# A graph network in one kernel: narrower count in layer 2, key tile, node parts, store and copies of the last layers

## The chip, the cores and the metric

One core of a Trainium2 chip runs the whole program in one launch. The metric is device microseconds from start to end of an execution; three executions give a median. One more execution was taken by the hardware profiler, and all rows below are from it.

## The reference

6250 nodes with 32 features, 200000 edges sorted by target. Four graph layers, each with a residual and a layer norm. Shapes come from the kernel's inputs.

```python
x = _layernorm(x + L0(x, edge_attr_32))     # relu(x[src] + e), summed over dst
x = _layernorm(x + L1(x))                   # cosine attention, softmax over dst
x = _layernorm(x + L2(x, edge_attr_2))      # spline convolution
x = _layernorm(x + L3(x, edge_attr_16))     # five PNA sub-layers
# L2: keys = row * 25 + idx[:, s]; four basis weights s, h summed by key, then
out = jnp.einsum('nki,kio->no', h, weight) / clip(deg, 1) + x @ root_weight + bias
# L3, five times, T = 4 towers of 8 features:
h = einsum(concat([xi, xj, ee]), pW) + pb   # xi = x[dst], xj = x[src], ee = edge_attr @ eW + eb
ssum = segment_sum(h, dst); cnt = segment_sum(1, dst)
mean = ssum / max(cnt, 1); mx = segment_max(h, dst), 0 where cnt is 0
x = relu(einsum(concat([xt, mean, ssum, mx]), poW) + pob) @ lW + lb)
```

Since h is linear in xi, xj and ee, the part of xi is the same for all edges of a target: the sum is cnt times it plus the sum of the rest, the maximum is it plus the maximum of the rest.

## The kernel before

Edges stand in 1568 columns of 128, in 28 chunks of 56 columns (C = 56, NCH = 28). Nodes stand in 49 columns of 128, in NGR = 7 groups of GR = 7. TensorE, VectorE, ScalarE, GpSimd and SyncE each run a program written out by hand; they meet at semaphores (`z3.at(...)`, `z2.at(...)`, `w3.at(...)`), and each engine works in the order of its code.

*Layer 2* (`layer2_t`, `layer2_v`): for each edge column, TensorE adds a message to one of 4 x 128 rows of nodes in four banks of PSUM: `L2096` multiplies a one-hot of the node's low part (written by ScalarE, L2105 and L2111) with MM, the message spread over the node's high part (written by VectorE, L2168, one operation for two columns; the message itself comes from L2142 to L2160, once in 14 columns). There are two halves of a number (high and low, p = 0, 1) and four banks, so 8 matmuls for an edge column. A row has F1 = 34 values: 32 features, a 1 that counts the degree, and a 0.

*Layer 3*: for each chunk, GpSimd gathers source rows from TQ for 32 columns (`layer3_g`, L2236) and TensorE picks the other columns with one-hots (`pick`, L2402, 8 matmuls a step; reduced by VectorE, L2587). One-hots of 4 key tiles come from VectorE (`one_hots`, L2581, one operation of 1536 keys for each tile) and are widened by ScalarE (L2499). Keys come by DMA (`key_block`, L636 to L641): KB on 128 partitions, and KM, in which the last 8 partitions hold other keys; KM serves tile 0, KB tiles 1 to 3. Rows are added (L2597) and scanned along the sorted targets (L2618), laid out by ScalarE (L2487) and stored to W by SyncE (`store`, L2277). A semaphore `landed` (L2271) lets GpSimd collect each node's last row from W (`node_rows`, L2220), and a scatter fixes rows at chunk borders (L2242) in TF, which SyncE loads into O3[1] (L2297).

*Node parts*: after the last chunk of a sub-layer, for each group of 7 columns, VectorE builds `z` (own x, mean, sum, maximum, 128 values, 8 operations L2628 to L2646), TensorE turns it (`turn_z`, L2380, 7 transposes), ScalarE copies it (L2469, L2471), TensorE multiplies it with AO (`mixed`, L2392, 7 products of 32 columns), VectorE adds CO and clips (L2653, L2657), TensorE turns the new x (L2352) and makes the two products of the next sub-layer (`products`, L2369), and VectorE writes PN, the part of xi, and QN, the part of xj (L2556, L2559), and halves it for picking (L1029, L1032). In the last sub-layer, the residual and layer norm follow (L2659 to L1067). `layer3_v` writes the groups interleaved: mixed(g), z(g+2), products(g-1), parts(g-1). The same products run for all groups ahead of the first sub-layer.

*Weights*: `weights3_t` and `weights3_v` (L1911, L1963) multiply the weights of the five sub-layers at the end of layer 1, 4 products each. *Set-apart rows*: `set_apart` (L643) copies 8 x 13 node rows into a tile from which 8 partitions of the picking operand are filled (L1037, L1039), at layer 1's start and ahead of each sub-layer.

## Time and profile before

| | us |
|---|---|
| median of 3 runs | 11380.92 (11370.02 to 11386.19) |
| the profiled execution | 11385.12 |
| its span, first to last instruction | 11383.4 |
| TensorE busy, mean granted clock | 10496.1 (92%), 0.964 |
| VectorE, ScalarE, GpSimd busy | 8222.9 (72%), 6684.8 (59%), 8086.8 (71%) |
| layer 2 | 2847 to 5244 |
| picks of the five sub-layers of layer 3 | from 5300.0, 6516.4, 7733.0, 8949.8 and 10161.6, each 1139.2 to 1139.6 long |
| between them | 77.2, 77.2, 77.2, 72.8 |
| after the last | 82 |

Busy time of an engine is a share of stages with different limits, so it is read stage by stage. In a timeline, a row is a run of equal instructions: its start, how long it lasted, engine, line, operation, output and inputs, the number of instructions, and in brackets the idle time ahead of it with what ended it. PE is TensorE, DVE VectorE, ACT ScalarE, POOL GpSimd, SPq the issue of DMAs by SyncE. PEclk is the granted clock, as a share of 2.4 GHz.

### The profile page before, as it was taken

The numbers are of one execution on the slowest core, as the hardware profiler recorded it, in microseconds if no ns is written. First come the engines' busy times: TensorE is split into PE (matmuls) and PEld (weight loads), VectorE is DVE, ScalarE is ACT, GpSimd is POOL, SyncE is SP. The second block draws the span as 40 slices with busy tenths as digits, with TensorE's granted clock in tenths as the row PEclk, the third lists the DMA queues.
The fourth block names the chain that finished last, engine by engine and source line by source line (L and its number), as shares of the span: only waits on it lengthen the run. The fifth ranks groups of instructions, "written<-read, shape, count | busy, mean of one in ns | idle before, by whom it ended". The sixth has DMA issues, their size and how long they took to land. (4 is left out here: it accounts for less than half of the span.)

```text
span 11383.4 us, 153184 instructions
## 1 busy us (share of the span) xinstructions
PE 10496.1 (92%) x55476; PEld 10002.9 (88%) x55476; DVE 8222.9 (72%) x11247; ACT 6684.8 (59%) x6615; POOL 8086.8 (71%) x8215
## 2 busy tenths in 40 slices
PE   4999859996999999998999899989999899989998
PEld 4999848885999999998999899989999899989997
DVE  5776658886888888887666666666666666666666
ACT  2443325554888888885655455554555455545554
POOL 3777777775666666664777677777777677767776
PEclk8999979997999999998999899999999899999998
DMA  7333234434333333332333333333333333333333
GB/s 225 124 115 113 81 66 101 101 100 125 88 89 85 85 89 85 84 88 63 113 110 108 93 108 108 108 108 93 108 109 110 92 110 110 109 93 109 108 108 90
DMA packets 672345, 1170.49 MB, mean 103 GB/s; under 512 B 200361, under 2 KB 458534, under 8 KB 652502
## 3 DMA queue, kind: packets, MB, share of 16 engines
q1 hardware_dynamic: 369098, 833.53, 22.1%
q0 software_dynamic: 287552, 293.65, 12.7%
q10 hardware_dynamic: 15384, 40.39, 1.1%
q14 instruction: 266, 2.18, 0.1%
q8 instruction: 45, 0.74, 0.0%
HBM read 786.62 MB, written 422.62 MB: 106 GB/s over the span
## 5 line engine op out<-in xcount | busy, mean ns | idle before, releaser
L2402 PE MATMUL ps<-qs,oh 128*128 128x416 f32 (+1 forms) x27200 | 5350.1, 352 | 136.9 <-ACT oh L2499 59.7
L2236 POOL DMA_INDIRECT l3g<-TQ,srcs x4440 | 4267.6, 961 | 1527.9 <-issue 1063.9
L2402 PEld LDWEIGHTS ps<-qs,oh 128*128 128x128 f32 x27200 | 4925.0, 188 | 408.8 <-DVE l3g L2587 208.9
L2587 DVE TENSOR_REDUCE l3g<-ps 128x32 f32<-128x416 f32 x3400 | 1918.2, 583 | 1592.0 <-PE ps L2402 1591.5
L2499 ACT CAST oh<-nd 128x1536 fp32r<-128x1536 bf16 x1140 | 1676.1, 1471 | 1727.6 <-DVE nd L2581 1727.6
L2096 PE MATMUL ps<-l2mm,l2oh 128*128 128x408 f32 (+1 forms) x12544 | 2389.9, 352 | 24.4 <-DVE l2mm L2168 24.4
L2096 PEld LDWEIGHTS ps<-l2mm,l2oh 128*128 128x128 f32 x12544 | 2332.7, 188 | 64.4 <-DVE l2mm L2168 25.2
L2080 POOL DMA_INDIRECT l2g<-Y,place x1568 | 1598.3, 1019 | 814.8 <-DVE l2mm L2168 398.7
L2168 DVE TENSOR_TENSOR l2mm<-l2hl,psv 128x1768 fp32r<-128x1768 f32 x784 | 1532.1, 1992 | 261.7 <-PE ps L2096 257.8
L2111 ACT ACTIVATE l2oh<-l2far,l2one 128x512 fp32r<-128x512 f16 x1568 | 1135.2, 724 | 292.6 <-PE ps L2096 290.2
L1211 POOL DMA_INDIRECT l0g<-T,srcs x896 | 968.2, 1081 | 422.5 <-issue 224.8
L1525 PE MATMUL ps<-qs,l1oh 128*128 128x442 f32 (+1 forms) x5376 | 1063.5, 358 | 215.9 <-issue 143.1
L1525 PEld LDWEIGHTS ps<-qs,l1oh 128*128 128x128 f32 x5376 | 998.8, 189 | 280.4 <-issue 143.2
L2618 DVE TENSOR_TENSOR_SCAN l3of<-l3mr,psv 128x912 f32<-128x912 bf16 x560 | 1145.6, 2047 | 9.7
L2487 ACT COPY l3o<-l3of 128x1792 f32<-128x1792 f32 x280 | 994.1, 3550 | 246.8 <-DVE l3of L2618 246.8
L2105 ACT ACTIVATE l2far<-l2line,nkey 128x512 f16<-128x512 f16 x1568 | 1108.9, 707 | 4.0 <-DVE l2one L2178 4.0
L1284 PE MATMUL ps<-qs,l0oh 128*128 128x416 f32 (+1 forms) x5376 | 1039.1, 352 | 58.9 <-DVE l0g L1370 46.0
L1284 PEld LDWEIGHTS ps<-qs,l0oh 128*128 128x128 f32 x5376 | 994.9, 192 | 71.9 <-DVE l0g L1370 53.0
L1456 POOL DMA_INDIRECT l1g<-T,srcs x896 | 858.5, 958 | 273.1 <-issue 222.2
L1623 ACT CAST l1oh<-nd 128x1024 fp32r<-128x1024 bf16 x336 | 341.5, 1049 | 536.9 <-DVE nd L1693 530.2
L2522 ACT COPY psv<-ps 128x512 f32<-128x512 f32 (+1 forms) x560 | 293.8, 525 | 502.0 <-PE ps L2413 502.0
L1370 DVE TENSOR_REDUCE l0g<-ps 128x32 f32<-128x416 f32 x672 | 385.6, 584 | 279.8 <-PE ps L1284 278.0
(423 smaller groups left out, 7310.3 us busy)
## 6 DMA issues: line engine op xcount, KB each, us to landing
W<-l3o SPq DMA_DIRECT2D x140, 1792.0 KB
mneg<-KG SPq DMA_DIRECT2D x280, 384.0 KB
l3km<-KG SPq DMA_DIRECT2D x280, 360.0 KB
l3g<-TQ,srcs POOLq DMA_INDIRECT x4440
l3t<-AT SPq DMA_DIRECT2D x140, 448.0 KB, 3.9
W<-l1o SPq DMA_DIRECT2D x28, 952.0 KB, 4.0
l0e<-U_a SPq DMA_DIRECT2D x28, 896.0 KB, 4.7
S<-RX SPq DMA_DIRECT2D x49, 512.0 KB
```

Source lines behind the costliest of these rows:

```text
L1284: x_ = e.matmul(ps[k % 3][:, 0:32 * n], OH0[k // SB0][:, g, 128 * (k % SB0):128 * (k % SB0) + 128], QS0[:, p, 32 * n0:32 * (n0 + n)], star ...
L1525: x_ = e.matmul(ps[r % 3][:, 0:F1 * n], rows[:, g, at:at + 128], QS1[:, p, F1 * n0:F1 * (n0 + n)], start=g == 0 and p == 0, stop=g == PG - ...
L2080: e.indirect_dma_start(G2[s3][:, j, :], None, cells, bass.IndirectOffsetOnAxis(ap=place[:, j0 + j:j0 + j + 1], axis=1)).then_inc(z2[f"g{s3 ...
L2096: x_ = e.matmul(ps[g][:, 0:F1 * n], OH2[:, q % C2, 128 * g:128 * g + 128], MM[:, q % R2, p, :, :].rearrange("e h f -> e (h f)")[:, 0:F1 * ...
L2105: e.activation(far[j % 4][:, :], line[:, :], ACT.Abs, bias=nkey[:, j:j + 1]).then_inc(z2["far"], 1)
L2111: e.activation(OH2[:, j % C2, :], far[j % 4][:, :], ACT.Relu, scale=-1.0, bias=unit[:, 0:1]).then_inc(z2["oh"], 1)
L2168: e.tensor_tensor(MM[:, r:r + 2, :, :, :].rearrange("p c k h f -> p (c k) h f"), HL[u % 2][:, 2 * t:2 * t + 2, :, None, :].rearrange("p c ...
L2236: e.indirect_dma_start(G3[s][:, j, :], None, TQ, bass.IndirectOffsetOnAxis(ap=srcs[:, c * C + j:c * C + j + 1], axis=0)).then_inc(z3[f"g{s ...
L2402: x_ = e.matmul(ps[(KPX * l + k) % 3][:, 0:32 * n], OH[(l + k // SB) % 2][:, g, 128 * (k % SB):128 * (k % SB) + 128], QS[:, p, 32 * n0:32 ...
L2499: e.copy(OH[m % 2][:, g, 0:w], OB[g % 2][:, 0:w]).then_inc(z3["oh"], 1)
L2587: e.tensor_reduce(G3[i % 3][:, C - KP + k if k < KP else C - KPE + k - KP, :], ps[r % 3][:, 0:32 * PH].rearrange("p (h f) -> p f h", f=32) ...
L2618: e.tensor_tensor_scan(OF[step][:, :, :].rearrange("p f j -> p (f j)")[:, x0:x1], MR[step][:, :, :].rearrange("p f j -> p (f j)")[:, x0:x1 ...
```

## The change

Layer 2: a row of MM for p = 0 is DG = 14 columns, a one-hot of the node's high part, and then 14 x 32 of the message; for p = 1 the 32-wide part alone. A new small operation writes the 14 columns; the product writes 4 x 416 elements. The degree is the sum in the first 14 columns of the banks.

Layer 3's keys: KM is filled on the last 32 partitions only (RIM = 96), and the one-hot of tile 0 is written by two operations, 32 partitions from KM and 96 from KB.

Set-apart rows: one copy in place of 8. Store: in a sub-layer's last chunk the store of the chunk before is issued ahead of the third key block, not behind it.

Node parts: the own part of x no longer goes through z. z is Zb + Fx and max(Zb, Fx), in place, 64 values; turn_z transposes two columns at once (4 transposes), and mixed multiplies pairs with a matrix AP of two copies of the weights (4 products of 128 columns; the last of 64). What comes of xi (own, cnt times, and where cnt is above 0) is made by a second set of products into another bank and put together in XA by five operations (`own_rows`). `mixed` on VectorE has a multiplication with rc and an addition of XA more. Weights: 11 products per sub-layer in place of 4; `mixer` and `matrices` write WR and AP for one sub-layer at a time.

```diff
+        def key_block_rim(e, kb, km, j0, n, rim_, signal):
+            rows = lambda t_, p: t_[j0:j0 + n, :].rearrange("(o j) p -> o (j p)", o=1).to_broadcast([p, 128 * n])
+            e.dma_start(kb, rows(KG, 128)).then_inc(signal, 16)
+            e.dma_start(km[rim_:LOW, :], rows(KG, LOW - rim_)).then_inc(signal, 16)
+            e.dma_start(km[LOW:LOW + 4, :], rows(KA, 4)).then_inc(signal, 16)
+            e.dma_start(km[LOW + 4:128, :], rows(KD, 4)).then_inc(signal, 16)
+
         def set_apart(e, rows, to, signal):
-            for p in range(8):
-                e.dma_start(to[13 * p:13 * p + 13, :], rows[LOW + p:LOW + p + 1, 0:13, :]).then_inc(signal, 16)
+            e.dma_start(to[0:104, :], rows[LOW:128, 0:13, :]).then_inc(signal, 16)
...
-                e.matmul(ps[2][:, 0:32], BO[:, l, :, :].rearrange("a b c -> a (b c)"), LW[:, l, :],
-                         start=True, stop=True).then_inc(w3["mm"], 1)
+                rest, mean, sum_, most, own_ = BO[:, l, 2:4, :], BO[:, l, 1, :], BO[:, l, 2, :], BO[:, l, 3, :], BO[:, l, 0, :]
+                for h in range(2):
+                    e.matmul(ps[2][64 * h:64 * h + 64, 0:32], rest.rearrange("a b c -> a (b c)"), LW[:, l, :],
+                             start=True, stop=True)
+                for h in range(2):
+                    e.matmul(ps[2][64 * h:64 * h + 32, 32:64], mean, LW[:, l, :], start=True, stop=True)
+                e.matmul(ps[2][0:32, 64:96], own_, LW[:, l, :], start=True, stop=True)
+                e.matmul(ps[2][0:32, 96:128], mean, LW[:, l, :], start=True, stop=False)
+                e.matmul(ps[2][0:32, 96:128], most, LW[:, l, :], start=False, stop=True).then_inc(w3["mm"], 1)
                 e.matmul(ps[3][:, 0:32], POB[:, l:l + 1].to_broadcast([32, 128]), LW[:, l, :],
                          start=True, stop=True).then_inc(w3["mm"], 1)
+                e.wait_ge(*w3.at("made", 5 * l + 3))
+                e.matmul(ps[4][0:32, 0:64], PT[:, l, :], A2[:, :, :].rearrange("p a b -> p (a b)"), start=True,
+                         stop=True).then_inc(w3["mm"], 1)
...
-                e.wait_ge(*w3.at("mm", 4 * l + 1))
-                e.tensor_tensor(WR[:, l, :, :], ps[0][:, None, 0:32].to_broadcast([128, 8, 32]),
-                                bm[:, :, None].to_broadcast([128, 8, 32]), ALU.mult).then_inc(w3["made"], 1)
-                e.wait_ge(*w3.at("mm", 4 * l + 2))
+                e.wait_ge(*w3.at("mm", 5 * l + 1))
+                e.tensor_copy(W5[:, l, :], ps[0][:, 0:32]).then_inc(w3["made"], 1)
+                e.wait_ge(*w3.at("mm", 5 * l + 2))
                 e.tensor_tensor(C0[:, l, :], ps[1][:, 0:32], PB[:, l, :], ALU.add).then_inc(w3["made"], 1)
-                e.wait_ge(*w3.at("mm", 4 * l + 3))
-                e.tensor_copy(AO[:, l, :], ps[2][:, 0:32]).then_inc(w3["made"], 1)
-                e.wait_ge(*w3.at("mm", 4 * l + 4))
+                e.wait_ge(*w3.at("mm", 5 * l + 3))
+                e.tensor_copy(AO[:, l, 0:32], ps[2][:, 0:32])
+                for h in range(2):
+                    e.tensor_copy(AO[64 * h:64 * h + 32, l, 32:64], ps[2][64 * h:64 * h + 32, 32:64])
+                e.tensor_copy(BX[:, l, 32:64], ps[2][0:32, 64:96])
+                e.tensor_copy(A2[:, 0, :], ps[2][0:32, 96:128])
+                e.tensor_copy(A2[:, 1, :], ps[2][0:32, 0:32]).then_inc(w3["made"], 1)
+                e.wait_ge(*w3.at("mm", 5 * l + 4))
                 e.tensor_tensor(CO[:, l, :], ps[3][:, 0:32], LB_[:, l, :], ALU.add).then_inc(w3["made"], 1)
+                e.wait_ge(*w3.at("mm", 5 * l + 5))
...
-                            x_ = e.matmul(ps[g][:, 0:F1 * n], OH2[:, q % C2, 128 * g:128 * g + 128],
-                                          MM[:, q % R2, p, :, :].rearrange("e h f -> e (h f)")[:, 0:F1 * n],
+                            x_ = e.matmul(ps[g][:, DG * p:DG + 32 * n], OH2[:, q % C2, 128 * g:128 * g + 128],
+                                          MM[:, q % R2, p, DG * p:DG + 32 * n],
...
-                e.tensor_tensor(MM[:, r:r + 2, :, :, :].rearrange("p c k h f -> p (c k) h f"),
+                e.tensor_tensor(MM[:, r:r + 2, 0, 0:DG], hpb[:, 2 * n:2 * n + 2, None].to_broadcast([128, 2, DG]),
+                                iot[:, None, 0:DG].to_broadcast([128, 2, DG]), ALU.is_equal)
+                e.tensor_tensor(MM[:, r:r + 2, :, DG:MW].rearrange("p c k (h f) -> p (c k) h f", f=32),
                                 HL[u % 2][:, 2 * t:2 * t + 2, :, None, :].rearrange("p c k o f -> p (c k) o f").to_broadcast(
-                                    [128, 4, PH, F1]),
+                                    [128, 4, PH, 32]),
                                 M5[u % 2][:, 2 * t:2 * t + 2, :, :, None].rearrange("p c k h o -> p (c k) h o").to_broadcast(
-                                    [128, 4, PH, F1]), ALU.mult).then_inc(z2["mk"], 1)
+                                    [128, 4, PH, 32]), ALU.mult).then_inc(z2["mk"], 1)
...
                     for m in range(blocks3(i) + 2, blocks3(i + 1) + 2):
+                        if m == blocks3(i) + 2 + NB3 and c:
+                            store(i - 1)
                         if m < blocks3(ALL3):
                             keys(m)
-                    if c:
+                    if 0 < c < NCH - 1:
                         store(i - 1)
...
+                    e.wait_ge(*z3.at("xa", k))
+                for w_, bank, done in ((WX[0], ps[5], z3["pq"]), (WX[1], ps[7], z3["px"])):
+                    for h, w in ((0, 4), (1, 3)):
+                        e.wait_ge(*z3.at("xts", 2 * k + h + 1))
+                        i = e.matmul(bank[:, 256 * h:256 * h + 64 * w], XT[s][0:32 * w, h, :], w_[0:32 * w, 0:64 * w],
+                                     start=True, stop=True)
...
+                for h in range(4):
+                    n = 64 * min(2, GR - 2 * h)
+                    m = e.transpose(ps[2 * (h // 2)][0:n, (h % 2) * 128:(h % 2) * 128 + 128],
+                                    O3[0][:, c0 + 2 * h:c0 + 2 * h + n // 64, :].rearrange("p c f -> p (c f)"), ident[:, :])
+                    if h % 2:
                         m.then_inc(z3["zt"], 1)
...
+            def own_rows(l, q):
+                c0, k = GR * ORD[q], NGR * l + q
+                c1, w = c0 + GR, [128, GR, 32]
+                pa, pb_ = (ps[b][:, 0:64 * GR].rearrange("p (a b) -> p a b", b=64) for b in (5, 7))
+                e.wait_ge(*z3.at("px", k + 1))
+                vc.up(e.tensor_tensor(XA[:, c0:c1, :], pa[:, :, 32:64], CO[:, l, None, :].to_broadcast(w), ALU.add).then_inc(vec, 1))
+                vc.up(e.tensor_tensor(nd[:, c0:c1, :], pb_[:, :, 0:32], has[:, c0:c1, None].to_broadcast(w), ALU.mult).then_inc(vec, 1))
+                a = vc.up(e.tensor_tensor(XB, pb_[:, :, 32:64], cnt[:, c0:c1, None].to_broadcast(w), ALU.mult).then_inc(vec, 1))
+                e.wait_ge(vec, a)
+                a = vc.up(e.tensor_tensor(nd[:, c0:c1, :], nd[:, c0:c1, :], XB, ALU.add).then_inc(vec, 1))
+                e.wait_ge(vec, a)
+                e.tensor_tensor(XA[:, c0:c1, :], XA[:, c0:c1, :], nd[:, c0:c1, :], ALU.add).then_inc(z3["xa"], 1)
 
...
+                    n = 128 if g else RIM
+                    if g == 0:
+                        e.tensor_scalar(OB[0][RIM:128, 0:w], KM[m % 2][RIM:128, 0:w], ramp[RIM:128, 0:1], None, ALU.is_equal)
+                    e.tensor_scalar(OB[g % 2][0:n, 0:w], KB[m % 2][0:n, 0:w], ramp[0:n, g:g + 1], None,
                                     ALU.is_equal).then_inc(z3["ob"], 1)
 
...
+                if k == 0:
+                    e.wait_ge(s_fx, 16 * (l + 1))
                 e.wait_ge(ngs[g], 16 * GR * (3 + l))
...
-                                ALU.mult).then_inc(z3["z"], 1)
+                e.tensor_tensor(Zb[:, c0:c1, 0:32], Zb[:, c0:c1, 0:32], Fx[:, c0:c1, 0:32], ALU.add)
+                e.tensor_tensor(Zb[:, c0:c1, 32:64], Zb[:, c0:c1, 32:64], Fx[:, c0:c1, 32:64],
...
+                a = vc.up(e.tensor_tensor(nd[:, c0:c1, :], pm[:, :, 32:64], rc[:, c0:c1, None].to_broadcast(w),
+                                          ALU.mult).then_inc(vec, 1))
+                e.wait_ge(vec, a)
+                e.tensor_tensor(nd[:, c0:c1, :], pm[:, :, 0:32], nd[:, c0:c1, :], ALU.add).then_inc(z3["masks"], 1)
                 e.wait_ge(*z3.at("masks", q + 1))
+                a = vc.up(e.tensor_tensor(nd[:, c0:c1, :], nd[:, c0:c1, :], XA[:, c0:c1, :], ALU.add).then_inc(vec, 1))
+                e.wait_ge(vec, a)
```

TensorE, one edge column of layer 2 (ps0 to ps3 are the banks, 128x442 the columns), before:

```order
L2096 MATMUL ps0<-l2mm,l2oh 128x442 x2
L2096 MATMUL ps1<-l2mm,l2oh 128x408 x2
L2096 MATMUL ps2<-l2mm,l2oh 128x408 x2
L2096 MATMUL ps3<-l2mm,l2oh 128x408 x2
```

and after:

```order
L2131 MATMUL ps0<-l2mm,l2oh 128x430
L2131 MATMUL ps0<-l2mm,l2oh 128x416
L2131 MATMUL ps1<-l2mm,l2oh 128x398
L2131 MATMUL ps1<-l2mm,l2oh 128x384
L2131 MATMUL ps2<-l2mm,l2oh 128x398
L2131 MATMUL ps2<-l2mm,l2oh 128x384
L2131 MATMUL ps3<-l2mm,l2oh 128x398
L2131 MATMUL ps3<-l2mm,l2oh 128x384
```

The number of matmuls is the same, with 140 columns fewer in all.

TensorE between two sub-layers, one group: turning z (l3g0, then l3o0), mixed, turning the new x (xc), the next sub-layer's products (hpb), before:

```order
L2380 MATMUL ps0<-ident,l3g0 128x128 x4
L2380 MATMUL ps1<-ident,l3g0 128x128 x3
L2369 MATMUL psv<-hpb,l3of0 128x256
L2369 MATMUL psv<-hpb,l3of0 128x192
L2392 MATMUL ps2<-ao,l3g1 128x32 x7
L2352 MATMUL ps3<-ident,xc 128x128
L2352 MATMUL psv<-ident,xc 96x128
```

and after:

```order
L2414 MATMUL ps0<-ident,l3o0 128x128 x2
L2414 MATMUL ps2<-ident,l3o0 128x128
L2414 MATMUL ps2<-ident,l3o0 64x128
L2403 MATMUL psv<-hpb,l3of0 128x256
L2403 MATMUL psv<-hpb,l3of0 128x192
L2403 MATMUL psv<-hpb,l3of0 128x256
L2403 MATMUL psv<-hpb,l3of0 128x192
L2428 MATMUL ps1<-hpb,l3g1 128x128 x3
L2428 MATMUL ps1<-hpb,l3g1 128x64
L2385 MATMUL ps3<-ident,xc 128x128
L2385 MATMUL psv<-ident,xc 96x128
```

The transposes and mixed products are fewer, the products of the next sub-layer twice as many, and order among the steps is the same.

VectorE there, from a group's mixed (L2653) to the halves of the group before (L1032), before:

```order
L2653 TENSOR_TENSOR nd<-ps2,co 128x224
L2657 TENSOR_SCALAR xc<-nd 128x224
L2628 COPY l3g0<-xc 128x7x32
L2629 TENSOR_TENSOR nd<-RX,cnt 128x224
L2633 TENSOR_TENSOR nd<-nd,l3o1 128x224
L2635 TENSOR_TENSOR nd2<-l3o1,l3o0 128x224
L2638 TENSOR_TENSOR nd2<-RX,nd2 128x224
L2641 TENSOR_TENSOR l3g0<-l3o0,nd 128x7x32
L2643 TENSOR_TENSOR l3g0<-nd2,has 128x7x32
L2646 TENSOR_TENSOR l3g0<-l3g0,rc 128x7x32
L2556 COPY RX<-psv 128x224
L2559 TENSOR_TENSOR l3of1<-psv,c0 128x224
```

and after:

```order
L2703 TENSOR_TENSOR nd<-ps1,rc 128x224
L2706 TENSOR_TENSOR nd<-ps1,nd 128x224
L2708 TENSOR_TENSOR nd<-nd,RX 128x224
L2711 TENSOR_SCALAR xc<-nd 128x224
L2694 TENSOR_TENSOR l3o0<-l3o0,l3o1 128x7x32
L2695 TENSOR_TENSOR l3o0<-l3o0,l3o1 128x7x32
L2609 TENSOR_TENSOR l3of1<-psv,c0 128x224
L1045 CAST qs<-l3of1 120x192
L1045 CAST qs<-l3of1 128x32
L1048 TENSOR_TENSOR qs<-l3of1,qs 120x192
L1048 TENSOR_TENSOR qs<-l3of1,qs 128x32
L2617 TENSOR_TENSOR RX<-psv,co 128x224
```

Four operations of own_rows follow behind the last of these (L2618 to L2623); work on the own part of x has moved from ahead of turn_z to behind the products.

## Rows read from the trace of the kernel before

**Rows 1.** Costliest groups: line engine op, out<-in xcount | busy, mean ns | idle before, releaser.

```profile
L2236 POOL DMA_INDIRECT l3g<-TQ,srcs x4440 | 4267.6, 961 | 1527.9 <-issue 1063.9
...
L2499 ACT CAST oh<-nd 128x1536 fp32r<-128x1536 bf16 x1140 | 1676.1, 1471 | 1727.6 <-DVE nd L2581 1727.6
L2096 PE MATMUL ps<-l2mm,l2oh 128*128 128x408 f32 (+1 forms) x12544 | 2389.9, 352 | 24.4 <-DVE l2mm L2168 24.4
```

**Rows 2.** Windows of stages: us, busy of each engine (x), PEclk, DMA share, GB/s.

```profile
2847.00:5244.00 2397.00, 2396.99 (x12737) 2355.19 (x12738) 2113.67 (x1625) 2092.04 (x3162) 1578.04 (x1548) 1.00 0.31 85
...
6516.00:7655.00 1139.00, 1114.84 (x5827) 1053.75 (x5828) 770.12 (x1122) 658.52 (x447) 857.03 (x892) 1.00 0.37 107
...
7656.00:7733.00 77.00, 40.82 (x197) 35.44 (x196) 47.13 (x121) 21.88 (x33) 44.42 (x46) 0.59 0.25 77
11301.00:11383.00 82.00, 36.11 (x154) 31.57 (x152) 57.16 (x151) 15.68 (x23) 37.05 (x38) 0.53 0.22 68
```

**Rows 3.** Waits of all engines: line <- releaser: us in total, times, longest.

```profile
DVE l3g L2587 <- PE ps L2402: 1591.5, 1684, 4.1
...
DVE l2mm L2168 <- PE ps L2096: 257.8, 309, 1.0
...
DVE psv L2597 <- issue: 180.2, 116, 2.3
```

**Rows 4.** Timeline of TensorE in layer 2: start, us, engine line op, count [idle before].

```profile
3907.98 34.33 PE L2096 MATMUL ps<-l2mm,l2oh 128*128 128x442 f32 x180
```

**Rows 5.** Timeline of VectorE: reduces behind picks in layer 1 and layer 3.

```profile
1564.16 0.60 DVE L1699 TENSOR_REDUCE l1g<-ps 128x33 f32<-128x429 f32 x1 [0.93 <-PE ps L1525]
1565.69 0.60 DVE L1699 TENSOR_REDUCE l1g<-ps 128x33 f32<-128x429 f32 x1 [0.93 <-PE ps L1525]
...
7041.38 0.59 DVE L2587 TENSOR_REDUCE l3g<-ps 128x32 f32<-128x416 f32 x1 [0.88 <-PE ps L2402]
7042.85 0.59 DVE L2587 TENSOR_REDUCE l3g<-ps 128x32 f32<-128x416 f32 x1 [0.88 <-PE ps L2402]
```

**Rows 6.** Timeline of VectorE in layer 2: four products in a row.

```profile
3956.38 7.71 DVE L2168 TENSOR_TENSOR l2mm<-l2hl,psv 128x1768 fp32r<-128x1768 f32 x4
```

**Rows 7.** Timeline of GpSimd in layer 3: gathers.

```profile
7001.26 0.94 POOL L2236 DMA_INDIRECT l3g<-TQ,srcs  x1 [0.30 <-issue]
7002.51 1.06 POOL L2236 DMA_INDIRECT l3g<-TQ,srcs  x1 [0.30 <-issue]
```

**Rows 8.** Timeline of VectorE beside those gathers.

```profile
7002.84 0.61 DVE L2581 TENSOR_SCALAR nd<-l3km,ramp 128x1536 bf16<-128x1536 f16 x1
```

**Rows 9.** Timeline of VectorE at layer 1's end: two sub-layers' weights.

```profile
2722.98 0.42 DVE L1969 TENSOR_TENSOR wr<-ps,RX 128x256 f32<-128x256 f32 x1 [0.72 <-PE ps L1916]
...
2725.18 0.42 DVE L1969 TENSOR_TENSOR wr<-ps,RX 128x256 f32<-128x256 f32 x1 [0.72 <-PE ps L1916]
```

**Rows 10.** Timeline of VectorE at layer 1's start.

```profile
1537.03 0.41 DVE L1037 CAST qs<-l1qd 128x34 fp32r<-128x34 f32 x1 [4.23 <-DMA l1qd<-l1n]
```

**Rows 11.** Timeline of TensorE at layer 3's start: two groups.

```profile
5282.93 1.86 PE L2369 MATMUL psv<-hpb,l3of 128*128 128x256 f32 x4 [0.35 <-DVE l3of L2559]
...
5285.57 1.86 PE L2369 MATMUL psv<-hpb,l3of 128*128 128x256 f32 x4 [0.35 <-DVE l3of L2559]
```

**Rows 12.** Timelines of SyncE, GpSimd and VectorE at the end of the second sub-layer.

```profile
7641.31 29.79 SPq L2277 DMA_DIRECT2D W<-l3o  x2
...
7677.03 0.99 POOL L2242 DMA_INDIRECT TF<-l3t,fixn  x1 [0.30 <-SPq L2271]
...
7685.80 0.39 DVE L2633 TENSOR_TENSOR nd<-nd,l3o 128x224 f32<-128x224 f32 x1 [13.96 <-DMA l3o<-TF]
...
7693.21 0.39 DVE L2653 TENSOR_TENSOR nd<-ps,co 128x224 f32<-128x224 f32 x1 [2.14 <-PE ps L2392]
```

**Rows 13.** Timeline of TensorE there, in a later group at half clock.

```profile
7711.84 1.75 PE L2380 MATMUL ps<-ident,l3g 128*128 128x128 f32 x7 [1.28 <-DVE l3g L2646]
...
7714.88 3.03 PE L2392 MATMUL ps<-ao,l3g 128*128 128x32 f32 x14
```

195 lines of the change are left out of this document (95 added, 100 removed).

## The prediction

> **What bounds the kernel now.** I read five views: the costliest groups, the busy time by stage, the waits, the timeline of each place that the diff touches, and the order of instructions before and after.
>
> The groups [rows 1] say where the mass is: layer 3's 4440 gathers with 4268 us on GpSimd, and layer 2's 12544 matmuls with 2390 us on TensorE; layer 3's picks are the rest of TensorE's time. The stages [rows 2] say what limits each. In layer 2, from 2847 to 5244, TensorE is busy in 2397 of 2397 us at clock 1.00 and VectorE in 2114 (88%): whatever shortens the matmuls shortens the stage, as long as VectorE fits. A layer-3 sub-layer takes about 1139 us, and there neither TensorE nor VectorE (770 us) is the whole story: the add L2597 waits for "issue" [rows 3], that is for gathers, which GpSimd starts 1.25 us apart [rows 7]. A chunk has 32 of them (4440 in 140 chunks), so 40.0 us of its 40.7 (1139/28) when no gather is lengthened; TensorE is busy 39.8 of them (1114.84/28). GpSimd is the bound, and TensorE stands less than 1 us below it. The node parts between sub-layers (77 us each, four times, and 82 at the end) are chains at half clock (0.59, 0.53) in which no engine is full: there single latencies count.
>
> **The change, part by part.**
>
> *Layer 2, narrower.* The rows of a message go from 34 to 32 wide and the count becomes 14 columns. Columns per edge column fall from 2x442 + 6x408 = 3332 to 430 + 416 + 3x398 + 3x384 = 3192. TensorE's step before is 8 matmuls: 34.33 us for 180 [rows 4] is 1.526 us for 8, or 1.519 when the last one's tail is left off. What 3192 columns take is read from two neighbours with the same eight-matmul pattern [rows 5]: layer 1 with 3400 columns steps by 1.53, layer 3 with 3200 by 1.47. So the new step is about 1.465, a gain of 0.045 to 0.063; I take 0.056, nearest to the layer-3 row. Over 1568 edge columns: **-88** (-71 to -99). VectorE must stay under it. Seven products and a message part fill 14 edge columns. A product takes 7.71/4 = 1.93 us [rows 6]; with 1664 in place of 1768 elements 1.82. The small one-hot write beside it (28 elements) I put at 0.11; bounds are 0.06 and 0.2, the shortest VectorE operations at the other places. So it breaks even, and 88% of 21.4 us is 18.8 of a new 20.5. The cover (257.8 us of waiting for TensorE [rows 3]) shrinks to about 170 and stays. ScalarE is busy 2092 us of 2397 [rows 2], 1.33 per edge column, below 1.465 as well; that is the thinnest cover.
>
> *One-hots of key tile 0.* One operation becomes two (32 partitions from the small tile, 96 from the full one), 285 more of about 0.6 us [rows 8]; the key DMA is smaller. VectorE has room (waits of 1591.5 us for TensorE in L2587 alone [rows 3]), so nothing of their own time counts. What counts is the gather beside them: at 7002.51 one takes 1.06 instead of 0.94 while the one-hot of 7002.84 runs [rows 7, 8]. Averaged: the gathers' mean is 961 ns against 940 undisturbed [rows 1, 7], 4440 x 0.021 = 93 us over 1140 one-hots [rows 1], 0.08 us each. 285 x 0.08 = 23, less those that fall into chunks bound by TensorE: **+20** (0 to +86, the latter if every added operation meets a gather at the worst phase, 0.3 us).
> By the Trainium skill, SBUF — State Buffer, section "SBUF: two separate sides", the port pair shared by VectorE and GpSimd is an exclusive lock held for the whole instruction, and the other engine "fully blocks". Taken so, each added operation would hold a gather for up to its own 0.61 us; the trace shows 0.12 in that pair, so the rule holds in kind and not in size. It speaks against this part and is the first rival.
>
> *Weights of layer 3, at layer 1's end.* A sub-layer's turn is 2.20 us (2722.98 to 2725.18 [rows 9]), 4 products and 4 VectorE operations. After: 11 products (+7 at about 0.21 us, 1.5), two more copies in series and a round trip through the last product and its copy (0.7 + 0.2 + 0.3), 5 short copies of 0.19 partly behind: 4.7 to 5.9, I take 5.2. 5 x 3.0 = **+15** (+12 to +19). Nothing beside hides it: the node gathers are ready and the next VectorE work waits for it.
>
> *Set-apart rows.* 8 DMAs become one. At layer 1's start VectorE waits 4.23 us for them [rows 10], and one still has to land beside the seven that go: **-4** (-4 to 0). At the start of layer 3 they stand ahead of the last stores of TQ in SP's queue; there the gain lies between 0 and the same 4, I take 2, counted below.
>
> *Layer 3's start.* Groups come 2.64 us apart [rows 11] at half clock. The 4 product records take 1.86. After, there are 8 (+1.7), and the next group's products wait until own_rows (5 operations of 0.39, as in rows 12, 1.9 us with their gaps) is done, which the old ones need not: 5.5 with the rest behind it shifted. Six gaps: +17, less the 2 of the set-apart rows: **+15** (+10 to +18).
>
> *Four ends between sub-layers.* The first z waits for the fix-up rows. SP's store L2277 is issued after the key blocks, at 7641.31; its landing lets the TF scatter go (7677.03, behind 21 node gathers on GpSimd) and the load, and z runs at 7685.80 [rows 12]. With the store one key block earlier, 4 issues, 1.7 us or so, this chain comes 1.7 to 2.6 earlier. Then z is 2 operations (0.65 us) in place of 6 behind the wait (2.3), four transposes in place of seven (1.75 us for seven at half clock [rows 13], so 1.0), so from z to the first mixed, 7.4 before [rows 12], about 4.1. Gained by then: 5 to 6. After it, each of seven groups: VectorE has 14 operations as before (8+2+4 before; 2+4+3+5 now), TensorE 1.0 + 3.5 + 1.9 (8 wider records at about 0.23) against 1.75 + 1.8 (products, as in rows 11) + 3.03 for 14 [rows 13]: 6.4 against 6.6 at half clock, no gain. At full clock VectorE binds, some 14 x 0.35 = 4.9 before and 5.2 after, since the operations added at the end wait for each other. The last group has own_rows behind it and products that wait for the own_rows before: +1 to +3. Net -4 each (-8 to +2): **-16** (-32 to +8).
>
> *Last end.* VectorE is busy 57 of 82 us [rows 2] there, and bounds it. The first mixed comes 3.4 earlier; five z of 8 operations shrink to 2 (8 x 0.37 = 3.0 to 0.65, -11.6); seven mixed grow by 2 operations (0.84 each, +5.9); the last wait for TensorE is 2 shorter: **-11** (-15 to 0).
>
> **Sum.** -88 + 20 + 15 - 4 + 15 - 16 - 11 = -69. The profiled run took 11385.1 in all, so 11316; the median of the runs is 4.2 below it: 11312. I say **11312**.
>
> **The rivals.**
> *1. The second one-hot stalls the gathers (ends slower).* Place: VectorE L2581 against GpSimd L2236, in the chunks bound by gathers. For it: the 1.06 beside the 0.94, and two such operations back to back hold twice as long. Against: the average of 0.08. Without this part the sum is -89; at a price of 0.31 us an operation the gain is gone, and at 0.39 the kernel is slower by over 0.2%. With 0.61, a gather held for the whole operation: -89 + 174 = +85, 11466. I give it 0.06.
> *2. Layer 2 doesn't shrink.* ScalarE (1.33 busy per edge column of 1.465) or VectorE takes over as the bound, or TensorE's step stays because something else than the columns, such as the loading of the 8 weights, sets it. For it: nothing in rows 4 alone excludes it. Against: layer 3 loads eight weights a step too and its step is 1.47 [rows 5]. Price: +88 gone, -69 + 88 = +19, 11400. Half of it gone gives 11356. 0.10 for the whole, within 0.2%.
> *3. The node parts cost more.* The chains of rows 12 and 13 are paid at half clock, and mixed now also needs AP and XA: if each end only comes out at +5 and the two starts at their upper ends, the sum is 40 higher, 11350, still faster. 0.10.
> *4. They gain more.* Less work at half clock, an early store that frees 5 us, one-hots at no cost: -60 more at most, around 11275. 0.12.
>
> **How the numbers follow.** Forecast 0.62, rivals 0.06, 0.10, 0.10, 0.12. Within 0.2% (23 us) is about what a measurement of this kernel can't tell from no change: 11358 to 11404. Faster: 0.62 + 0.10 + 0.12 = 0.84; same 0.10; slower 0.06. The range for 8 in 10: from 11268 (layer 2 at -99, four ends at -32 and free one-hots together give -69 - 11 - 16 - 20 = -116, which is 11265) to 11356 (layer 2 at half its gain).
>
> **What would show it.** Layer 2: a run of matmuls at 0.183 us each where it is 0.190, stage 2397 to about 2309, VectorE's wait for TensorE smaller. Picks of a sub-layer: 1139 to about 1143, mean of L2236 up from 961 to about 965. Layer-1 end +15, layer-3 start +15, middle gaps 77 to 73, last end 82 to 71. It would be wrong if layer 2 stays above 2350, if gathers' mean goes above 980, or if the gaps grow.

## The result and the profile after

Median 11352.84 us of 14 runs (11345.69 to 11359.97) against 11381.7 of 14 runs of the kernel before: ratio 0.9975, 95% interval 0.9967 to 0.9983, so 29 us faster (19 to 38). The forecast was 69 us faster, 11312, with a range up to 11356. The direction was right, the gain less than half. The profiled execution has a span of 11353.0 us.

Stage by stage, with the lengths read from the traces (from the start of the first matmul to the start of the last, in layer 2 and in the picks of each sub-layer; what lies between):

| stage | before | after | measured | forecast |
|---|---|---|---|---|
| layer 1's last pick to layer 2 | 158.3 | 164.3 | +6.0 | +15 |
| layer 2 | 2397.4 | 2319.0 | -78.4 | -88 |
| layer 2 to the first pick of layer 3 | 55.6 | 66.9 | +11.3 | +15 |
| picks of the five sub-layers | 5696.8 | 5771.6 | +74.8 | +20 |
| four gaps between them | 304.4 | 275.2 | -29.2 | -16 |
| from the last pick to the end | 82.2 | 73.2 | -9.0 | -11 |

These add up to -24.5 of the span's -30.4. The rest lies ahead of layer 2, where the stages differ by more than that between executions that have the same code there (below).

The costliest groups of the kernel after (columns as in [rows 1]):

```profile
L2438 PE MATMUL ps<-qs,oh 128*128 128x416 f32 (+1 forms) x27200 | 5354.7, 352 | 195.9 <-DVE l3g L2653 119.7
L2267 POOL DMA_INDIRECT l3g<-TQ,srcs x4440 | 4343.3, 978 | 1536.8 <-issue 1101.3
...
L2131 PE MATMUL ps<-l2mm,l2oh 128*128 128x384 f32 (+3 forms) x12544 | 2311.6, 346 | 24.5 <-DVE l2mm L2205 24.5
...
L2647 DVE TENSOR_SCALAR nd<-mneg,ramp 96x1536 bf16<-96x1536 f16 (+1 forms) x1140 | 703.8, 617 | 72.4 <-ACT oh L2537 67.9
```

The gathers' mean went from 961 to 978 ns, where 965 was forecast, and VectorE's one-hots are 1140 again in this row with 285 more in the row of L2646. 4440 x 0.017 = 75 us is just what the sub-layers grew by. The 12544 matmuls of layer 2 have 78 us less.

The windows of its stages (columns as in [rows 2]):

```profile
2847.00:5166.00 2319.00, 2318.87 (x12739) 2301.64 (x12740) 2103.98 (x2409) 2088.48 (x3162) 1585.74 (x1548) 1.00 0.32 88
6455.00:7607.00 1152.00, 1116.42 (x5830) 1054.57 (x5831) 812.88 (x1184) 658.00 (x447) 877.74 (x900) 1.00 0.31 92
7607.00:7677.00 70.00, 35.04 (x165) 28.05 (x164) 47.19 (x123) 19.35 (x40) 37.35 (x40) 0.71 0.26 81
11280.00:11353.00 73.00, 24.98 (x90) 18.18 (x88) 47.72 (x123) 13.77 (x30) 36.06 (x38) 0.52 0.25 76
5166.00:5233.00 67.00, 24.88 (x75) 18.49 (x73) 44.23 (x111) 12.43 (x22) 0.00 (x0) 0.58 0.13 36
```

Layer 2 is still all TensorE (2318.87 of 2319), and VectorE's 88% has become 91%: it remained under. A sub-layer has TensorE busy 1116, as before, in a window 13 longer: the growth is idle time. The gap's granted clock is 0.71 in place of 0.59.

The waits (columns as in [rows 3]):

```profile
DVE l3g L2653 <- PE ps L2438: 1459.9, 1496, 2.3
...
PEld ps L2438 <- DVE l3g L2653: 288.2, 502, 1.3
...
DVE l2mm L2203 <- PE ps L2131: 184.7, 211, 1.0
```

VectorE waits 132 us less for picks. TensorE's weight loads wait 288.2 for VectorE's reduces, 208.9 before.

### The profile page after: what moved, and what is told of

The parts are those of the page before. It is cut to its first block and busy times, and to the rows that moved or that the text cites. A ratio compares the mean times of both kernels' runs of the same rounds, so it can differ in the third digit from the quotient of the medians.

```text
span 11353.0 us, 154077 instructions
## 1 busy us (share of the span) xinstructions
PE 10393.5 (92%) x55371; PEld 9905.4 (87%) x55371; DVE 8419.2 (74%) x12358; ACT 6665.9 (59%) x6650; POOL 8166.0 (72%) x8215
## 5 line engine op out<-in xcount | busy, mean ns | idle before, releaser
L2267 POOL DMA_INDIRECT l3g<-TQ,srcs x4440 | 4343.3, 978 | 1536.8 <-issue 1101.3
L2438 PEld LDWEIGHTS ps<-qs,oh 128*128 128x128 f32 x27200 | 4922.3, 188 | 474.8 <-DVE l3g L2653 288.2
L2653 DVE TENSOR_REDUCE l3g<-ps 128x32 f32<-128x416 f32 x3400 | 1903.4, 582 | 1459.9 <-PE ps L2438 1459.9
L2131 PE MATMUL ps<-l2mm,l2oh 128*128 128x384 f32 (+3 forms) x12544 | 2311.6, 346 | 24.5 <-DVE l2mm L2205 24.5
L2131 PEld LDWEIGHTS ps<-l2mm,l2oh 128*128 128x128 f32 x12544 | 2279.1, 188 | 40.6 <-DVE l2mm L2205 25.3
L2205 DVE TENSOR_TENSOR l2mm<-l2hl,psv 128x1664 fp32r<-128x1664 f32 x784 | 1474.0, 1880 | 0.0
L2647 DVE TENSOR_SCALAR nd<-mneg,ramp 96x1536 bf16<-96x1536 f16 (+1 forms) x1140 | 703.8, 617 | 72.4 <-ACT oh L2537 67.9
```

The source lines that it names most:

```text
L2131: x_ = e.matmul(ps[g][:, DG * p:DG + 32 * n], OH2[:, q % C2, 128 * g:128 * g + 128], MM[:, q % R2, p, DG * p:DG + 32 * n], start=False, st ...
L2205: e.tensor_tensor(MM[:, r:r + 2, :, DG:MW].rearrange("p c k (h f) -> p (c k) h f", f=32), HL[u % 2][:, 2 * t:2 * t + 2, :, None, :].rearra ...
L2267: e.indirect_dma_start(G3[s][:, j, :], None, TQ, bass.IndirectOffsetOnAxis(ap=srcs[:, c * C + j:c * C + j + 1], axis=0)).then_inc(z3[f"g{s ...
L2438: x_ = e.matmul(ps[(KPX * l + k) % 3][:, 0:32 * n], OH[(l + k // SB) % 2][:, g, 128 * (k % SB):128 * (k % SB) + 128], QS[:, p, 32 * n0:32 ...
L2653: e.tensor_reduce(G3[i % 3][:, C - KP + k if k < KP else C - KPE + k - KP, :], ps[r % 3][:, 0:32 * PH].rearrange("p (h f) -> p f h", f=32) ...
```

## The experiments

### What the second one-hot costs, and why

In the kernel after, GpSimd's gathers and VectorE's one-hots in two places of the second sub-layer (timelines of each engine; start, us, engine line op):

```profile
7008.36 1.18 POOL L2267 DMA_INDIRECT l3g<-TQ,srcs  x1 [0.30 <-DVE l3g L2653]
7009.85 1.02 POOL L2267 DMA_INDIRECT l3g<-TQ,srcs  x1 [0.30 <-issue]
7011.17 1.22 POOL L2267 DMA_INDIRECT l3g<-TQ,srcs  x1 [0.31 <-DVE l3g L2653]
...
7029.26 1.32 POOL L2267 DMA_INDIRECT l3g<-TQ,srcs  x1 [0.30 <-DVE l3g L2653]
7030.88 0.94 POOL L2267 DMA_INDIRECT l3g<-TQ,srcs  x1 [0.30 <-issue]
...
7008.80 0.62 DVE L2646 TENSOR_SCALAR nd<-l3km,ramp 32x1536 bf16<-32x1536 f16 x1
7009.43 0.62 DVE L2647 TENSOR_SCALAR nd<-mneg,ramp 96x1536 bf16<-96x1536 f16 x1
...
7029.14 0.62 DVE L2646 TENSOR_SCALAR nd<-l3km,ramp 32x1536 bf16<-32x1536 f16 x1
7029.77 0.62 DVE L2647 TENSOR_SCALAR nd<-mneg,ramp 96x1536 bf16<-96x1536 f16 x1
```

The pair that starts at 7008.80 lasts until 7010.05, 1.25 us without a gap, as long as gathers stand apart. The gather of 7008.36 takes 1.18, the next 1.02; that of 7011.17, with 1.22, already stands beside the next tile's one-hot. Beside the pair of 7029.14 one takes 1.32. In [rows 7, 8] a single one-hot cost one gather 0.12. In this trace 433 of the 4440 gathers take over 1.14 us, in that of before 48.

**One operation again.**

```diff
-                    if g == 0:
-                        e.tensor_scalar(OB[0][RIM:128, 0:w], KM[m % 2][RIM:128, 0:w], ...)
-                    e.tensor_scalar(OB[g % 2][0:n, 0:w], KB[m % 2][0:n, 0:w], ...)
+                    e.tensor_scalar(OB[g % 2][:, 0:w], (KB if g else KM)[m % 2][:, 0:w], ...)
-                key_block_rim(...)
+                key_block(...)
```

> The changed kernel with key tile 0's one-hot in one operation again and KM filled on all 128 partitions (1140 one-hots, not 1425). Theory A, the back-to-back pair of VectorE operations lengthens gathers and the gathers bound the chunk: the five sub-layers fall from 1152 to 1157 us back to 1139 to 1141 each, the gathers' mean from 978 to about 961 ns, the whole to about 11353 - 75 = 11278. Theory B, the sub-layers grew through other new work (weights per sub-layer, store order, node parts) or the lighter key DMA moved the phase: they stay above 1148 and the whole above 11330.

Measured: 11274.68 us (4 runs), ratio to before 0.9909 (0.9893 to 0.9926). The sub-layers take 1136.3 to 1139.1, together 5692.2, which is 79.4 less than in the kernel after. The gathers are back at 961:

```profile
L2267 POOL DMA_INDIRECT l3g<-TQ,srcs x4440 | 4267.5, 961 | 1536.5 <-issue 1064.2
```

Theory A holds, and within 4 us of the time: 11278 was expected.

**The split alone, in the kernel before.**

```diff
+                    if g == 0:
+                        e.tensor_scalar(OB[0][RIM:128, 0:w], KM[m % 2][RIM:128, 0:w], ...)
...
-                key_block(...)
+                key_block_rim(...)
```

> The kernel before with only the split of tile 0's one-hot and the narrower key fill. Theory A: +70 to +80 over five sub-layers (each 1139 to about 1154), about 11456 in all, gathers' mean 975 to 980 ns. Theory B: within 15 us of the kernel before.

Measured: 11445.08 (2 runs), ratio 1.006 (1.004 to 1.008). Sub-layers 1153.4 to 1156.2, together 5774.0, +77.2:

```profile
L2244 POOL DMA_INDIRECT l3g<-TQ,srcs x4440 | 4344.9, 979 | 1526.0 <-issue 1100.4
```

This split is slower than the kernel before on its own, lighter key DMA (72 KB in place of 360) included. No run has the lighter DMA with a single one-hot, so the two are bounded together by the next run and not told apart.

The traces say at which one-hots the gathers lose the time. A gather far from any one-hot takes 0.944 us. What the others take above it, added up by the one-hots beside them (those that start from 0.62 us ahead of a gather's start to 0.6 us behind it), is 32.9 us beside tile 0's and 44.0 beside those of tiles 1 to 3 with one operation, and 71.4 and 78.0 in the kernel after; before and with the split alone it is 35.4 and 41.6 against 71.6 and 79.3. So about half of the loss stands at the pair, and as much at the single one-hots behind it, which now start at other moments of a gather.

**The same two operations, not side by side.** The 32-partition one is issued two picks earlier.

```diff
                         one_hots(..., k < KP)
+                        if k < KP and k % SB == 0:
+                            rim_part(blocks3(i) + k // SB + 1)
```

> The changed kernel with the 32-partition one-hot operation issued one picking step and a half earlier than the 96-partition one, so that no two such operations stand back to back (but for 6 of 285). If it is the pair's length (1.24 us, as long as the spacing of gathers) that always hits a gather, each single operation costs the 0.07 to 0.08 us of an average one: sub-layers 1143, the whole about 11353 - 55 = 11298. If every operation of this kind costs 0.26 us wherever it is put, nothing changes: sub-layers 1152 to 1157, 11353.

Measured: 11295.5 (4 runs), ratio 0.9929 (0.9912 to 0.9945). Sub-layers together 5715.6, that is 56.0 below the kernel after and 23.4 above the run with one operation, 0.082 us for each of 285. The VectorE rows show them 2.9 us apart, and the gathers' mean is 963:

```profile
7011.39 0.82 DVE L2657 TENSOR_SCALAR nd<-l3km,ramp 32x1536 bf16<-32x1536 f16 x1
...
7014.33 0.62 DVE L2647 TENSOR_SCALAR nd<-mneg,ramp 96x1536 bf16<-96x1536 f16 x1
```

```profile
L2267 POOL DMA_INDIRECT l3g<-TQ,srcs x4440 | 4275.8, 963 | 1537.8 <-issue 1134.6
```

The pair costs 79.4/285 = 0.28 us, and most of it is the price of standing back to back. That the lone operation comes out at the forecast's 0.08 is chance, though. From a sub-layer's first gather to its last the five take 5619.6 us with one operation, 5628.5 here and 5694.8 in the kernel after: the lone operations, with the lighter key DMA, cost the gathers 8.9 us, 0.03 each. The other 14.3 lie behind the last gather, which is followed by the last pick 15.3 us later in every sub-layer with one operation and in the kernel after, and here 16.6 to 20.5; why is open. And VectorE pays too: the 0.82 above stands where 0.62 is usual. In this trace 475 one-hots start 0.5 to 0.6 us behind a gather's start; they take 0.78 us on average, and the gathers beside them their usual 0.944.

**VectorE as busy, but with reduces from PSUM.**

```diff
                 e.wait_ge(*z3.at("pk", r + 1))
+                if k < KP and SPREAD[k % SB] == (0,) or k >= KP and SPREADX[k % SB] == (0,):
+                    e.wait_ge(vec, vc.n)
+                    vc.up(e.tensor_reduce(spare[:, :], ps[r % 3]..., AXX, ALU.max).then_inc(vec, 1))
```

> The kernel before with 285 of the reduces behind the picks (those of the steps at which tile 0's one-hot is written) made twice, the first time into a spare tile: 285 more VectorE operations of 0.58 us, read from PSUM, in the place of the second one-hot operation. Theory A (VectorE and GpSimd meet at a port that the 16-bit SBUF operation holds): nothing to +10 us, gathers' mean 961 ns. Rival C (VectorE is late for its reduces, so picks and chunk are late): +60 to +80, sub-layers at 1152 or more.

Measured: 11367.33 (8 runs), ratio 0.9993 (0.9983 to 1.0003). The sub-layers are 1137.0 to 1137.6 long, 2 less than before, and the gathers' mean is 959:

```profile
L2237 POOL DMA_INDIRECT l3g<-TQ,srcs x4440 | 4256.5, 959 | 1524.1 <-issue 1082.5
```

Rival C falls: 0.58 us more of VectorE at the same place, ahead of the reduce that TensorE waits for, cost nothing. What costs is the kind of operation, a 16-bit compare from SBUF to SBUF, against GpSimd's gathers; which of these properties does it, no run separates. The trace of before says the same of single gathers: 2603 run beside a reduce and away from any one-hot, and the longest of them takes 0.96 us. By the Trainium skill, SBUF — State Buffer, section "SBUF: two separate sides", a VectorE operation in a 2-port mode and one of GpSimd share a port pair, and whichever starts first holds it for its whole instruction while the other blocks. The runs agree in kind: reduces don't delay a gather, one-hots do, and a gather can delay a one-hot (the 0.82 above). In size they don't agree. In the trace of before, sorted by when a one-hot starts against the gather's own start, gathers take 944 ns where it starts 0.5 us or more ahead or 0.5 us or more behind, 1.065 us where it starts 0.3 to 0.4 us behind or ahead, and 1.17 to 1.24 us (means) where it starts 0.1 to 0.3 us ahead. Where it starts 0 to 0.25 us behind, 157 times, the gather takes 0.947 us and the one-hot its usual 0.61 to 0.62: side by side, and neither waits.

**Two operations, together no longer than one and a third.** Halves of the columns in place of parts of the partitions.

```diff
+                    if g == 0:
+                        e.tensor_scalar(OB[0][:, 0:w // 2], KM[m % 2][:, 0:w // 2], ...)
+                    h = 0 if g else w // 2
+                    e.tensor_scalar(OB[g % 2][:, h:w], (KB if g else KM)[m % 2][:, h:w], ...)
```

> The changed kernel with KM filled on all partitions and tile 0's one-hot in two operations of 128 partitions and half the columns each: 285 operations more as in the changed kernel, but together hardly longer than the one. If the length of the stretch in which VectorE runs such operations without a gap sets the price, the sub-layers stay at 1139 to 1141 (sum 5692 to 5710) and the whole at 11275 to 11292. If it is the number of operations, the sum is 5715 (0.08 us each) to 5772 (0.28 each).

> Tile 0's one-hot in two halves once more, for its time beside the run with all four in halves: 11267 by its first profile, against 11275 with one operation. Within 11260 to 11275 if the 16 us of the sub-layers are real; 11275 to 11285 if they were chance.

Measured: the first time 11266.57 in the profiled execution; a second execution took 30832 us, far off every other of any kernel here, and is left out. Repeated: 11266.64 (4 runs, 11260.96 to 11268.14), ratio 0.9902 (0.9886 to 0.9919). The sub-layers together are 5676.0 and 5674.3 in the two profiles. By group, and the two halves by shape:

```profile
L2267 POOL DMA_INDIRECT l3g<-TQ,srcs x4440 | 4249.4, 957 | 1536.9 <-issue 1061.1
...
L2647 DVE TENSOR_SCALAR nd<-l3km,ramp 128x768 bf16<-128x768 f16 x280 | 131.2, 469 | 0.0
...
L2645 DVE TENSOR_SCALAR nd<-l3km,ramp 128x768 bf16<-128x768 f16 x280 | 115.2, 412 | 0.9 <-DMA l3km<-KD 0.9
```

So the number of operations is not what costs. The two halves start 0.33 us apart and end some 0.8 us after the first began, against 1.24 for the full pair. That the sub-layers are 16 to 18 us shorter than with a single operation was not expected; two profiles show it, and the two medians differ by 8 us with intervals that overlap. It comes from tile 0: counted as above, the gathers beside its one-hots lose 2.4 and 2.7 us in these two profiles, where they lose 32.9 with one operation, and those beside tiles 1 to 3 lose 55.8 and 57.4, 12 to 13 more. Why the halves miss the gathers is open.

**All four tiles in halves.**

```diff
+                    for h in (0, w // 2):
+                        i_ = e.tensor_scalar(OB[g % 2][:, h:h + w // 2], ...)
+                    i_.then_inc(z3["ob"], 1)
```

> The changed kernel with KM filled on all partitions, and the one-hots of all four tiles in two operations of half the columns, 1140 more operations than with one each. Halving tile 0's alone brought the sum of the sub-layers from 5692 to 5676 us and the gathers' mean from 961 to 958 ns. If a short operation rarely covers the moment at which a gather needs the port, the mean falls to about 950 and the sum to 5640 to 5660, the whole to 11240 to 11260. Rival: the gain on tile 0 was chance of phase, and the sum stays within 5676 to 5700.

Measured: 11274.13 (4 runs), ratio 0.991 (0.9893 to 0.9927), sub-layers together 5688.6. The sum is the rival's, 5676 to 5700: nothing that can be told from noise is gained on the single operation (5692.2), and the gain of the halved tile 0 doesn't extend to the others. No gather takes over 1.2 us now, but more are lengthened a little, and their mean is 960:

```profile
L2267 POOL DMA_INDIRECT l3g<-TQ,srcs x4440 | 4261.8, 960 | 1537.0 <-issue 1043.6 <-DVE l3g L2652 308.4 <-DMA TQ<-l3of 185.1
...
L2645 DVE TENSOR_SCALAR nd<-mneg,ramp 128x768 bf16<-128x768 f16 x1680 | 637.9, 422 | 70.2 <-ACT oh L2537 70.2
```

### Between the sub-layers

In the kernel after, the first and last z of the second gap, and GpSimd's first node gather and its last:

```profile
7635.04 0.39 DVE L2694 TENSOR_TENSOR l3o<-l3o 128x224 f32<-128x224 f32 x1 [11.62 <-DMA l3o<-TF]
...
7659.65 0.39 DVE L2694 TENSOR_TENSOR l3o<-l3o 128x224 f32<-128x224 f32 x1 [0.45 <-DMA l3o<-W,lastq]
...
7592.33 0.94 POOL L2251 DMA_INDIRECT l3o<-W,lastq  x1 [0.30 <-issue]
...
7657.01 1.12 POOL L2251 DMA_INDIRECT l3o<-W,lastq  x1 [0.31 <-issue]
```

The node gathers start 15.0 us ahead of the last pick (5.4 before), since SP's `landed` no longer stands behind the third key block, and the last one is issued at 49.7 in place of 57.3 after it. The last z still waits 0.45 us for it in this gap. The forecast had seen only the first z move.

**The late store again.**

```diff
-                        if m == blocks3(i) + 2 + NB3 and c:
-                            store(i - 1)
-                    if 0 < c < NCH - 1:
+                    if c:
                         store(i - 1)
```

> The changed kernel with one one-hot operation for tile 0 (as in the run before this one, 11275 us) and the store of a sub-layer's last chunk but one issued behind the third key block again. If the early store is worth what the first z shows (30.0 us after the picks before the change, 27.8 after it), four gaps grow by 2.3 us each, +9, and the scatter goes back from 14.1 to 21.2 us after the picks. Rival: the gaps' gain is all of the shorter node parts, and they stay at 68 to 73 us.

Measured: 11305.77 (2 runs), ratio 0.9933 (0.9913 to 0.9953); gaps 76.0, 76.3, 81.0, 75.8 against 68.0, 72.6, 68.1, 69.0 with the early store: 7.9 each, where 2.3 was expected. (The 81.0 and the 72.6 each hold 4 to 5 us of another kind, which the next run shows.) VectorE's z rows of the second gap:

```profile
7615.35 0.39 DVE L2689 TENSOR_TENSOR l3o<-l3o 128x224 f32<-128x224 f32 x1 [13.19 <-DMA l3o<-TF]
...
7635.92 0.39 DVE L2689 TENSOR_TENSOR l3o<-l3o 128x224 f32<-128x224 f32 x1 [0.54 <-DMA l3o<-W,lastq]
...
7645.29 0.39 DVE L2689 TENSOR_TENSOR l3o<-l3o 128x224 f32<-128x224 f32 x1 [4.28 <-DMA l3o<-W,lastq]
```

Late, the first z comes 1.8 us later, and the last one 6.9 us, and ahead of it VectorE stands 4.28 us for the last node gathers.

**Eight copies again.**

```diff
-            e.dma_start(to[0:104, :], rows[LOW:128, 0:13, :]).then_inc(signal, 16)
+            for p in range(8):
+                e.dma_start(to[13 * p:13 * p + 13, :], rows[LOW + p:LOW + p + 1, 0:13, :]).then_inc(signal, 16)
```

> The changed kernel with one one-hot operation for tile 0, and the set-apart rows copied by 8 DMAs again. If the single copy is worth something, VectorE's wait ahead of the first one-hot of layer 1 goes back from 1.98 to 4.2 us, the stretch ahead of layer 3's picks grows from 66.5 to 68 or 69, and the four gaps by 0 to 2 each; rival: other waits cover it, and no stage moves by more than 1 us. Layer 1's own start and length differ by up to 15 us from run to run in the profiles so far, so layer 1 says nothing on this.

Measured: 11284.03 (2 runs), ratio 0.9914 (0.9894 to 0.9933); gaps 73.3, 72.9, 73.3, 73.6, so 3.9 each above 69.4; layer 3's start 66.8, unchanged. SyncE's issues in the second gap:

```profile
7644.31 6.26 SPq L662 DMA_DIRECT2D l3qd<-l3of  x8
7650.62 1.92 SPq L2282 DMA_DIRECT2D TQ<-l3of  x2
```

The eight take 6.26 us of issue, the one copy 0.74. That looks like the cause of the longer gaps, since the stores of the last two groups' TQ, which the first gather of the next sub-layer waits for, stand behind them. But the first gather isn't late. TensorE's first pick and GpSimd's first gather of that sub-layer, with eight copies and then with one:

```profile
7658.99 2.39 PE L2439 MATMUL ps<-qs,oh 128*128 128x416 f32 x6 [6.21 <-issue]
7654.20 0.94 POOL L2268 DMA_INDIRECT l3g<-TQ,srcs  x1 [17.42 <-DMA TQ<-l3of]
...
7649.13 3.37 PE L2438 MATMUL ps<-qs,oh 128*128 128x416 f32 x9 [5.94 <-issue]
7644.41 0.94 POOL L2267 DMA_INDIRECT l3g<-TQ,srcs  x1 [17.31 <-DMA TQ<-l3of]
```

With eight copies the first gathers start 68.5, 68.1, 69.0 and 68.8 us after the last pick, with one 68.0, 67.9, 68.7 and 69.0. What is late is the first pick, which starts 4.4 to 4.8 us behind the first gather where it usually starts with it, and it waits for no DMA: TensorE's branch into the loop of the chunks (L2463) lasts 5.1 to 5.4 us in the trace, and 0.4 where the pick comes on time. The same happens once with one copy, in the second gap (4.9 us, the second pair of rows), and altogether in 7 of the 28 gaps of the seven profiles with one copy and the early store. A sub-layer behind such a branch is 2 to 3 us shorter in its picks, since its gathers are already under way. So the copies cost a gap 0.2 us by its first gather, and the forecast, which gave them nothing there, was right; the 2 us that it gave them at layer 3's start were not there. Why the branch is slow in all four gaps here, and whether the copies have a part in it, is open. The whole, 9 us longer, has an interval that overlaps that of the run with one copy. VectorE's wait at layer 1's start goes back to 4.23 us, as expected.

**Neither.** Both edits together.

> The changed kernel with one one-hot operation for tile 0, the late store and the eight copies: of the parts that act between sub-layers only the node parts are left. If the parts add up (late store +7.9 a gap, eight copies +3.9, from 69.4), the gaps are 81 and the node parts alone make each gap 6 longer than the 75 of the kernel before. Rival: store and copies share one wait, so that the gaps stay at the 76 to 77 of the late store alone and the node parts alone cost 1 to 2.

Measured: 11314.02 (2 runs), ratio 0.9945 (0.9925 to 0.9965); gaps 76.4, 77.8, 76.6, 77.8, mean 77.2. The number is the rival's, but not for its reason. The 81 was added up with 3.9 for the copies, which was the branch; all four branches are short here (0.4 to 0.9 us). Read at the first gather, the four runs give these means of the four gaps:

| | late store | early store |
|---|---|---|
| eight copies | 77.2 | 68.6 |
| one copy | 76.2 | 68.4 |

So the store is worth 8 to 9 us a gap and the copy 0.2 to 1, whichever comes first. The node parts alone lengthen a gap by 1 to 3 us (77.2 against 76.1 in the first profile of before, 75.2 with the reduces made twice and 74.0 with the split alone, whose key DMA is lighter).

**The early store alone, in the kernel before.** The edit is the reverse of the one above.

> The kernel before with the early store alone. GpSimd's node gathers start 10 us earlier (-15.0 from the last pick in place of -5.4) and the last one ends its issue at 50 in place of 57. If the last groups waited for those gathers before as well, the gaps fall from 75 (72 to 77) to 67 to 70, the whole by some 25. Rival: in the old node parts VectorE's z and TensorE's products set the second half of a gap, so only the first z's 2.3 us are gained: gaps 73 to 75, the whole -9 or less.

Measured: 11369.12 (8 runs), ratio 0.9993 (0.9983 to 1.0003); gaps 70.5, 73.9, 70.7, 74.1, mean 72.3. Some 2 to 4 us a gap, little beyond the first z's 2; that is nearer to the rival's 73 to 75 than to the 67 to 70 first expected. In the old node parts the last z comes at 59.4 after the last pick, 9.5 behind the last node gather, so VectorE and TensorE set the pace there. The 8 us are to be had only with the new node parts, which with the late store stand 3.6 to 4.3 us waiting for the last node gathers.

### Layer 3's start

**own_rows ahead of the halves.**

```diff
                 products(0, g)
-                parts(0, g)
                 own_rows(0, g)
+                if g < NGR - 1:
+                    parts(0, g)
```

> The changed kernel with one one-hot operation for tile 0, and at layer 3's start own_rows ahead of the halves for the first six groups, since the next group's products wait for own_rows. If that wait sets the cadence there (4.6 us a group), the stretch from layer 2's last matmul to the first pick falls from 66.5 by 6 x 0.3 to 6 x 0.7, to 62 to 65. Rival: TensorE's eight records and the copies set it, and it stays. The whole is 11273, which can't be told from 11275.

Measured: 11272.7 (4 runs), ratio 0.9903 (0.9886 to 0.9919); the start 66.3, unchanged. The rival holds. TensorE's products come at the same distance, 5.30 us:

```profile
5206.43 3.33 PE L2403 MATMUL psv<-hpb,l3of 128*128 128x256 f32 x8 [1.55 <-DVE RX L2623]
...
5211.73 3.32 PE L2403 MATMUL psv<-hpb,l3of 128*128 128x256 f32 x8 [1.55 <-DVE RX L2623]
```

The halves had fitted into the time in which the second set of products runs; own_rows waits for that set in either order. The kernel after has the same pattern, with 1.55 us of waiting for own_rows in each group:

```profile
5204.29 3.33 PE L2403 MATMUL psv<-hpb,l3of 128*128 128x256 f32 x8 [1.55 <-DVE RX L2623]
...
5209.60 3.33 PE L2403 MATMUL psv<-hpb,l3of 128*128 128x256 f32 x8 [1.55 <-DVE RX L2623]
```

## Why the forecast was wrong

*The one-hots: wrong, and the step that failed.* "285 x 0.08 = 23 [...] **+20** (0 to +86 [...])". Measured +75 to +79. The term has the right mechanism, a gather held by a one-hot beside it, and a price that doesn't fit these operations. 0.08 us was an average over all one-hots (with the 0.944 us of the undisturbed gathers, not 0.94, it is 76/1140 = 0.067). Inside that average, tile 0's single one-hot already lengthens a gather in 266 of 280 cases, by 0.12 us, and those of tiles 1 to 3 in 311 of 824 gathers beside them. The new operation stands right behind tile 0's. Together they fill the distance between two gathers; the gathers beside them lose twice as much, and the one-hots of the other tiles are moved to moments at which they cost twice as much too. The sub-layers grow by 0.28 us for each pair, and by 0.082 when its two operations stand apart, of which the gathers account for 0.03. The pair was named in the rival ("two such operations back to back hold twice as long") but given 0.06 and priced at 0.61; even the bound of +86 was in the text. What was missing is the question whether an average of lone operations holds for a pair, and for the others once their place moves. This step is 55 to 59 us off, more than the 41 by which the median missed the forecast; the other terms together gave the rest back.

*Layer 2: right in mechanism, size off by 10.* -78.4 for -88, inside -71 to -99. A long run of matmuls after, to be read against [rows 4]:

```profile
3879.70 58.73 PE L2131 MATMUL ps<-l2mm,l2oh 128*128 128x430 f32 x320
```

58.73/320 = 0.1835 us. Over all of layer 2, steps of 0.3 us or more left out, the mean spacing went from 0.1897 to 0.1834, so 0.050 us in 8 and not 0.056: the step of before was read from one run as 1.519 and is 1.517, the one after was read from a neighbour as 1.463 and is 1.467. Two small errors of the same sign, times 1568. 140 columns are worth 0.36 ns each. Rival 2 fell. VectorE's wait in this stage (184.7) came out near the 170 named.

*Weights: right in sign, a third of the size.* +6.0 between the two profiles, +15 forecast; the stage is 158.0 to 159.3 us long in four profiles with the old code and 161.6 to 165.5 in ten with the new. VectorE's rows of one turn:

```profile
2716.24 0.19 DVE L1998 COPY w<-ps 128x32 f32<-128x32 f32 x1 [0.72 <-PE ps L1933]
...
2718.95 0.21 DVE L2011 COPY bx<-psv 32x64 f32<-32x64 f32 x1 [0.41 <-PE psv L1948]
2719.88 0.19 DVE L1998 COPY w<-ps 128x32 f32<-128x32 f32 x1 [0.72 <-PE ps L1933]
```

A turn is 3.64 us and not 5.2. The seven new products on 32 or 64 rows take 0.92 us from the first's start to the next one behind them, 0.13 each and not the 0.21 put in for all of them, and VectorE's short copies start 0.1 us apart.

*Set-apart rows at layer 1's start.* VectorE's wait fell by 2.3, from 4.23 [rows 10] to 1.98, where 4 was forecast with bounds of 0 and 4:

```profile
1536.84 0.18 DVE L1053 CAST qs<-l1qd 128x34 fp32r<-128x34 f32 x1 [1.98 <-DMA l1qd<-l1n]
```

With eight copies in the changed kernel it is 4.23 again, and with one copy in the run with one operation 0.94. No gain can be read from the stage: layer 1's first pick lies between 1536.8 and 1561.0 us and its picks last 1126.6 to 1142.7 in fourteen profiles, without order by code.

*Layer 3's start.* +11.3 for +15, inside its bounds. The cadence is 5.3 at half clock as worked out (5.5), but some groups run at full clock.

*Ends between the sub-layers.* -29.2 for -16, inside -32 to +8, by other causes than named, so that the nearness owes something to luck. The forecast gave the shorter path to the first mixed 3.3 us, the store 1.7 to 2.6, and the last group a loss of 1 to 3. By the first gathers, the node parts alone add 1 to 3 us a gap, and the early store takes 8 to 9 off them, since all of GpSimd's node gathers move with it and not the first z alone. The copy, given nothing, is worth 0.2 to 1. Store and node parts hang together: in the old node parts the store is worth 2 to 4.

*Last end.* -9.0 for -11.

## What to carry to other kernels

A price per operation that is averaged over a trace holds for operations that stand as they stood there. Here two back to back, as long as the period of the other engine's work, doubled the loss and moved the operations behind them to worse moments; keeping them apart, or the two together short, avoided it. An early transfer is to be followed on every queue that waits for it, and its worth is read behind the last of its users, not at the first. And a stretch between two stages is read on each engine that starts the next one: the picks' start alone charged a slow branch to the copies.

The best version measured is the change with tile 0's one-hot in one operation or in two halves of the columns: 11274.68 and 11266.64 us, 0.9909 and 0.9902 of the kernel before.

## What the runs showed of the hardware

285 reduces of 0.58 us from PSUM on VectorE cost GpSimd's gathers nothing (959 ns on average against 961). 285 more 16-bit compares of 0.62 us cost the five stretches of gathers 75 us where each stood right behind another, and 9 us, with the lighter key DMA, where they stood 2.9 us apart. Either side can be the one that waits: a gather takes up to 1.33 us in place of 0.944 beside a one-hot, and a one-hot that starts 0.5 to 0.6 us behind a gather's start 0.78 in place of 0.61. In the rows shown an operation on 32 partitions took as long as one on 96, 0.62 us for 1536 columns; half the columns took 0.41 us alone and 0.33 us to the next one's start. Fewer partitions saved no time here, and a halved row less than half. TensorE's branch into a loop took 0.4 us in most cases and 4.9 to 5.4 in others of the same code.
